# Routing stages: logits by expert in four column tiles, five place products a group, attention rows added one group further ahead

## What is computed

```python
xr = layernorm(x).reshape(-1, 256)
gate = softmax(xr @ Wg, axis=-1)                     # Wg: 256 x 16
idx = argmax(gate, axis=1)
gates_s = take_along_axis(gate, idx[:, None], axis=1)[:, 0]
onehot = one_hot(idx, 16)
loc = sum((cumsum(onehot, axis=0) - 1) * onehot, axis=1)
valid = loc < C                                      # C = 16384 / 16 = 1024
dispatched = zeros((16, C + 1, 256)).at[idx, minimum(loc, C)].set(xr)
```

## Time and profile before

| | us |
|---|---|
| median of 3 runs | 6074.56 |
| lowest and highest run | 6066.26, 6075.16 |
| profiled execution | 6057.65 |
| its span (first to last instruction) | 6056.0 |

### The profile page before, as it was taken

One profiled execution on the slowest core, in us unless ns is written; L12 is line 12 of the kernel. 1 busy time (PEld: TensorE's weight loads), 2 busy tenths in 40 slices (PEclk: granted clock), 3 DMA queues, 4 the chain that ended last, 5 costly groups with the idle time before them and its releaser, 6 DMA issues. The chain is left out here.

```text
span 6056.0 us, 128330 instructions
## 1 busy us (share of the span) xinstructions
PE 5607.2 (93%) x48544; PEld 3845.4 (63%) x48544; DVE 4586.8 (76%) x7474; ACT 3562.4 (59%) x5349; POOL 1574.0 (26%) x2093
## 2 busy tenths in 40 slices
PE   7888867999998979999999999999999997899998
PEld 5666656999987834444444444444444446799998
DVE  6888877556556768888888888888888884755554
ACT  5666533333324547777777777777777775333332
POOL 4666634333330000111111111111111114533333
PEclk9999967999999979999999999999999997799999
DMA  1111184222218921111111111111111113222221
GB/s 49 43 48 48 39 240 125 93 84 85 84 64 284 334 102 45 56 56 55 56 56 57 57 55 56 56 55 55 57 57 56 56 45 95 68 87 83 86 89 56
DMA packets 315523, 495.82 MB, mean 82 GB/s; under 512 B 36314, under 2 KB 221028, under 8 KB 311024
## 3 DMA queue, kind: packets, MB, share of 16 engines
q1 hardware_dynamic: 290544, 425.73, 22.0%
q0 software_dynamic: 24576, 64.56, 3.3%
HBM read 321.82 MB, written 168.82 MB: 81 GB/s over the span
## 5 line engine op out<-in xcount | busy, mean ns | idle before, releaser
L1672 DVE TENSOR_REDUCE at_best<-at_psM 128x2 f32<-128x1024 f32 x2048 | 2409.7, 1220 | 344.7 <-PE at_psM L1716 344.4
L1628 ACT ACTIVATE at_p<-at_psE 128x1024 f32<-128x1024 f32 (+1 forms) x2688 | 2067.7, 819 | 593.0 <-PE at_psE L1732 556.6
L1732 PE MATMUL at_psE<-at_q,at_k 50*128 50x512 f32 x4096 | 1125.8, 428 | 85.0 <-ACT at_p L1628 83.3
L1716 PE MATMUL at_psM<-at_k,at_q 48*128 48x512 f32 x4096 | 1097.5, 455 | 48.0 <-DMA at_v<-scratch_v 26.8
L1742 PE MATMUL at_psO<-at_p,at_v 128*17 128x256 f32 x16384 | 1087.2, 383 | 0.0
L1732 PEld LDWEIGHTS at_psE<-at_q,at_k 50*128 50x128 f32 x4096 | 557.4, 186 | 493.0 <-ACT at_p L1628 245.6
L1053 ACT ACTIVATE e_h_hi<-e_psH 128x512 fp32r<-128x512 f32 x512 | 306.5, 599 | 920.7 <-PE e_psH L90 767.8
L1127 DVE SCALAR_TENSOR_TENSOR e_h_lo<-e_psH,e_h_hi 128x512 fp32r<-128x512 f32 x512 | 353.9, 691 | 602.8 <-ACT e_h_hi L1053 532.4
L1742 PEld LDWEIGHTS at_psO<-at_p,at_v 128*17 128x17 f32 x16384 | 377.8, 97 | 558.8 <-issue 331.5
L1716 PEld LDWEIGHTS at_psM<-at_k,at_q 48*128 48x128 f32 x4096 | 493.5, 187 | 361.6 <-DVE at_best L1672 172.3
L90 PE MATMUL e_psE<-e_w_hi,e_h_hi 128*128 128x256 f32 x2048 | 582.7, 285 | 0.0
(11 more groups left out here) (192 smaller groups left out, 8820.9 us busy)
## 6 DMA issues: line engine op xcount, KB each, us to landing
e_w_raw<-in_w SPq DMA_DIRECT2D x64, 1024.0 KB
scratch_qk<-cp_qkh SPq DMA_DIRECT2D x64, 512.0 KB
scratch_qk<-cp_qkl SPq DMA_DIRECT2D x64, 512.0 KB
at_q<-scratch_qk SPq DMA_DIRECT2D x256, 128.0 KB
at_k<-scratch_qk SPq DMA_DIRECT2D x256, 128.0 KB
scratch_v<-cp_va SPq DMA_DIRECT2D x32, 544.0 KB
at_v<-scratch_v SPq DMA_DIRECT2D x128, 136.0 KB
a_x<-in_x SPq DMA_DIRECT2D x32, 512.0 KB
```

The lines of the kernel that those rows point to most:

```text
L1628: nc.scalar.activation(P[:, u:u + n, :], src, ACT.Exp, scale=HD ** -0.5).then_inc(p_ready, 1)
L1672: nc.vector.reduce_max(best[j % 2][:, h, :, qt], psM[h][:], AX_X).then_inc(m_taken, 1)
L1716: last = nc.tensor.matmul(psM[h][:, a, :], Q[j][r, 128 * qt:128 * qt + 128], K[j][r, 512 * h:512 * h + 512], start=True, stop=True)
L1732: last = nc.tensor.matmul(psE[:, u - u0 if n == 2 else 2, :], K[j][r, 128 * kc:128 * kc + 128], Q[j][r, 512 * half:512 * half + 512], star ...
```

## The change

It touches `routing_stage` only.

- **Logits by expert.** `by_expert` takes the 32 columns of `wg` (16 and 16 zeros) as weights and moves 256 tokens' columns of `r_xT`, for four quarters of the group, each into its own 32 partitions of a new bank `r_psE`: 8 products in place of 16. ScalarE copies `r_psE` to `r_logits_by_expert` (`take_by_expert`), and two transposes bring it back to tokens by experts in `r_psL`, now one buffer in place of two. The tiles of a group then lie as j and half h, and VectorE reads them through a rearranged view. In ScalarE's loop the copy stands first, ahead of `r_expd`; in TensorE's loop the two transposes stand behind the places.
- **Five place products.** VectorE adds tiles in pairs, pairs in fours and fours to the group's count (`r_pairs`, `r_quads`, `r_count`, all in bf16), and the tiles' counts reach later tiles by three products in place of seven.
- **Attention rows.** `add_attention` of group g+5 is done in one piece behind `choose` of g; only the bn_stats of g+4 are left between its steps, one after each.
- The weights `Wg` are loaded last of the first loads, into a tile that GpSimd has cleared.

```diff
@@ buffers
-        wg = sb("wg", [128, 2, E], F32)
+        wg = sb("wg", [128, 2, 32], F32)
+        logits_by_expert = sb("logits_by_expert", [128, G // 4], F32)
...
-        psL = [ps(f"psL{s}", [128, TI, E]) for s in range(2)]
+        psE = ps("psE", [128, G // 4])
+        psL = ps("psL", [128, 2, TI // 2, 32])
@@ SP
-            sp.dma_start(wg[:], Wg.rearrange("(k p) e -> p k e", p=128)).then_inc(wg_loaded, 16)
...
             for q in range(XB):
                 load(q)
+            sp.wait_ge(wg_clear, 1)
+            with nc.allow_non_contiguous_dma(reason="256 rows of 16 weights, once"):
+                sp.dma_start(wg[:, :, 0:E], Wg.rearrange("(k p) e -> p k e", p=128)).then_inc(wg_loaded, 16)
@@ ScalarE
+            def take_by_expert(q):
+                act.wait_ge(by_expert_done, q + 1)
+                after(act, logits_done, q)
+                nc.scalar.activation(logits_by_expert[:], psE[:], ACT.Copy).then_inc(by_expert_taken, 1)
+
             for g in range(-3, NG):
+                if here(g + 1):
+                    take_by_expert(g + 1)
                 if here(g):
@@ VectorE, choose
-                seq.did(nc.vector.tensor_reduce(count[:], onehot[s][:].rearrange("p t e -> p e t"), AX_X, ALU.add))
                 ahead(4)
                 seq.wait(g)
+                two = lambda v: v.rearrange("p (m c) e -> p m c e", c=2)
+                seq.did(nc.vector.tensor_tensor(pairs[:], two(onehot[s][:])[:, :, 0], two(onehot[s][:])[:, :, 1], ALU.add))
+                ahead(5)
+                seq.wait(g)
+                seq.did(nc.vector.tensor_tensor(quads[:], two(pairs[:])[:, :, 0], two(pairs[:])[:, :, 1], ALU.add))
+                ahead(6)
+                seq.wait(g)
+                seq.did(nc.vector.tensor_tensor(count[:], quads[:, 0], quads[:, 1], ALU.add))
+                ahead(7)
+                seq.wait(g)
                 nc.vector.tensor_tensor(counted[1 - s][:], counted[s][:], count[:], ALU.add).then_inc(onehot_ready, 1)
-                ahead(5, 6, 7)
@@ VectorE, loop
-            for g in range(-4, NG):
+            for g in range(-4 if att is None else -5, NG):
...
+                if att is not None and here(g + 5):
+                    add_attention(g + 5)
@@ TensorE
+            def by_expert(q):
+                pe.wait_ge(xT_ready, q + 1)
+                after(pe, by_expert_taken, q)
+                for k in range(2):
+                    for j in range(4):
+                        last = nc.tensor.matmul(psE[32 * j:32 * j + 32, :], wg[:, k, :], xT[q % 2][:, k, G // 4 * j:G // 4 * j + G // 4],
+                                                start=k == 0, stop=k == 1)
+                last.then_inc(by_expert_done, 1)
...
             def logits(q):
-                pe.wait_ge(xT_ready, q + 1)
-                after(pe, below_ready, q - 1)
...
+                pe.wait_ge(by_expert_taken, q + 1)
+                after(pe, below_ready, q)
+                for h in range(2):
+                    last = nc.tensor.transpose(psL[:, h], logits_by_expert[:, 128 * h:128 * h + 128], T.ident[:])
```

More of the change, by code:

```diff
@@ L576, in routing_stage @@
     CE = C // 128
+    assert TI == 8 and E == 16
     assert C % 128 == 0 and N % G == 0 and CH <= 256
@@ L784, in choose @@
                 dve.wait_ge(logits_done, g + 1)
[L785 to L786 removed]
+                by_tile = psL[:].rearrange("p h j e -> p j h e")[:, :, :, 0:E]
+                halves = lambda v: v[:].rearrange("p (j h) -> p j h", h=2)
+                seq.did(nc.vector.reduce_max(halves(mx), by_tile, AX_X))
+                ahead(0)
                 seq.wait(g)
                 after(dve, exp_ready, g)
[L789 to L790 removed]
+                nc.vector.tensor_tensor(below[:].rearrange("p (j h) e -> p j h e", h=2), by_tile,
+                                        halves(mx).unsqueeze(3).broadcast_to([128, TI // 2, 2, E]), ALU.subtract).then_inc(below_ready, 1)
+                ahead(1)
                 dve.wait_ge(below_ready, g + 1)
@@ L794, in choose @@
                                                        op0=ALU.is_equal, op1=ALU.mult))
-                ahead(1)
+                ahead(2)
                 seq.wait(g)
                 seq.did(nc.vector.reduce_max(best[:], marks[:], AX_X))
-                ahead(2)
+                ahead(3)
                 seq.wait(g)
@@ L836, in encode @@
                                         place_row[:].unsqueeze(2).broadcast_to([128, TI, 128]), ALU.is_equal).then_inc(in_row_ready, 1)
-            for g in range(-4, NG):
+            for g in range(-4 if att is None else -5, NG):
                 def ahead(*ts):
                     for t in ts:
-                        if here(g + 4) and t < TI:
+                        if here(g + 4):
                             measure(g + 4, t)
@@ L847, in _ @@
                 else:
-                    ahead(*range(-1, TI))
+                    ahead(*range(TI))
+                if att is not None and here(g + 5):
+                    add_attention(g + 5)
                 if here(g + 4):
@@ L883, in places @@
                 after(pe, codes_ready, g)
-                nc.tensor.matmul(psC[:], earlier[:], onehot[g % 2][:], start=True, stop=False, skip_group_check=True)
-                for t in range(TI - 1):
-                    nc.tensor.matmul(psC[:, t + 1:, :], ones[:], onehot[g % 2][:, t:t + 1, :].broadcast_to([128, TI - 1 - t, E]),
-                                     start=False, stop=False, skip_group_check=True)
+                part = dict(stop=False, skip_group_check=True)
+                hot = onehot[g % 2]
+                nc.tensor.matmul(psC[:], earlier[:], hot[:], start=True, **part)
+                nc.tensor.matmul(psC[:, 4:8], ones[:], quads[:, 0:1].broadcast_to([128, 4, E]), start=False, **part)
+                nc.tensor.matmul(psC[:].rearrange("p (a b c) e -> p a b c e", a=2, b=2)[:, :, 1], ones[:],
+                                 pairs[:].rearrange("p (a b) e -> p a b e", a=2)[:, :, 0].unsqueeze(2).broadcast_to([128, 2, 2, E]), start=False, **part)
+                nc.tensor.matmul(psC[:].rearrange("p (m c) e -> p m c e", c=2)[:, :, 1], ones[:],
+                                 hot[:].rearrange("p (m c) e -> p m c e", c=2)[:, :, 0], start=False, **part)
                 nc.tensor.matmul(psC[:], ones[:], counted[g % 2][:].unsqueeze(1).broadcast_to([128, TI, E]),
@@ L901, in _ @@
                 if here(g + 1):
-                    logits(g + 1)
+                    by_expert(g + 1)
                 if here(g):
                     places(g)
+                if here(g + 1):
+                    logits(g + 1)
                 if here(g + 2):
```

49 lines of the change are left out of this document (19 added, 30 removed).

## The result

| | before | changed |
|---|---|---|
| median, us | 6065.69 (6 runs, 6060.29 to 6075.16) | 6006.71 (6 runs, 6000.92 to 6018.13) |
| profiled execution, its span | 6057.65, 6056.0 | 6003.23, 6001.4 |
| mean granted clock | 0.961 | 0.967 |

The ratio is 0.9902 with a 95% interval of 0.9888 to 0.9916: 59 us faster, where 42 were forecast. 6006.7 lies 9 us under the lower end of the range, so the forecast was right in direction and too small.

What follows compares the result with a forecast made beforehand. VectorE was taken to bound r1 and TensorE r2. Savings of 14.8 us in r1 and 27.5 in r2, together 42.4, came off the median of 6074.56: 6032 us, range 6016 to 6056.

Steps and rivals of the forecast that it cites:

- The burst by expert: TensorE, both routing stages: eight products in four overlapping column tiles take 1.0 us a group in place of 3.64.
- the end of r_picked's wait: VectorE in r2: r_picked no longer waits for the places, taking 1.52 us out of the group's period.
- r_marks and r_onehot: VectorE, both stages: these two-input reads now wait for GpSimd's r_entry products, at 1.2 us each.
- the sixth load: Start of r1: group 1 now stands behind the adds of a sixth load, which lands at 830.8.
- TensorE's need in r2: Per group: table 4.1, burst 1.0, places 0.5, transposes back 0.4, other transposes 3.3, together 9.3 us.
- r2's start: Filling of r2: the first three groups no longer wait for slow logits, so group 2's maxima come 9.6 us earlier.
- both drains: Last three groups of each stage: 9.0, 9.0 and 8.3 us, gaining 5.0 us in r1 and 6.6 in r2.
- r2's tail: Stretch behind r2's last group: 0.15 us longer than before.
- The two periods, 12.5 and 9.95: VectorE's time per group in r1 and r2: 1.3 and 1.15 us less than before.
- r1's fill: Start of r1: the maxima of group 1 come 6.9 us later, at 837.4 in place of 830.56.
- mishaps (tiles, DMA, held reads): Rivals: column tiles don't overlap, 6052 us, chance 0.10; r1 stays at 13.8 through late rows or held reads, 6045, 0.08.
- The rival with the low clock: More idle time keeps TensorE at 1.2 GHz, needing 13.4 us a group; about 35 us slower, 6108 us, chance 0.04.

Runs made afterwards that it cites:

- no_rows_ahead: Changed kernel with the attention additions put back where the kernel before has them; 6021.8 us, ratio 0.9930.
- one_statistic_earlier: On no_rows_ahead, each of the eight bn_stats one place earlier in VectorE's row; 6025.1 us (1 run).
- statistics_early: Changed kernel with a group's eight row statistics issued earlier in VectorE's row, same work; 6001.1 us, run again 5991.6 us.
- narrow_burst: Changed kernel with the old 16 products of 16 columns added behind the logits by expert, result unread; 6100.8 us, ratio 1.0060.
- by_expert_alone: Kernel before with only the logits by expert in four column tiles, ScalarE's copy and two transposes back; 6026.3 us, ratio 0.9939.
- five_places_alone: Kernel before with only the sums of pairs and fours and five place products in place of nine; 6063.8 us, ratio 0.9996.
- rows_ahead_alone: Kernel before with only the eight attention additions together behind the choice, one group further ahead; 6049.6 us, ratio 0.9971.
- filled_chain: On statistics_early, the eight aggregations stand two by two between the four short additions, same work; 6001.9 us, ratio 0.9900.

## Why the prediction was too small

**What held.** Both mechanisms did: the earlier trace rows named the right engine in each stage. The burst by expert (1.0 forecast, 1.07), the two transposes (0.4, 0.39), the copy by ScalarE (0.4, 0.39), the end of r_picked's wait, r_marks and r_onehot (1.2, 1.12 and 1.15), adds that no longer wait, and the sixth load (830.8 forecast, its adds start at 829.22) were right. The rule read from the earlier trace rows, that an instruction of VectorE with two SBUF inputs waits for the end of GpSimd's product, was confirmed three times by moving work around it (no_rows_ahead, one_statistic_earlier, statistics_early). The Trainium skill ("SBUF — State Buffer", SBUF: two separate sides) calls it an exclusive lock. The rows agree: in the earlier trace rows the two products end at 917.43 and what stands behind the held add starts at 917.64, and in the changed kernel (897.06 and 3.85 long, so 900.91) the bn_stats behind r_onehot starts at 900.98.

**What failed, by terms.** The step that failed is the cost of TensorE's other work in r2, which I took at the clock of the kernel before; the second is a pair of periods that were each 0.4 us too long. The saving was 16.6 us short (59.0 against 42.4). The median of before, off which I took it, was 8.9 lower in six runs than in the three that I had, which is the draw of the runs and no step of the argument; taken off the later median, the range would have begun at 6007. Together that makes some 25 us. By the traces the terms were 17.6 short:

- *TensorE's need in r2, "4.1 + 1.0 + 0.5 + 0.4 + 3.3 = 9.3".* It took the table and the transposes at the clock that the earlier trace rows show (0.80 in the group), which the removed burst had held down, as narrow_burst shows by putting it back. Measured 6.80: the burst 1.07, places and the two transposes back 0.4 from start to start where I had 0.5 and 0.4, the transposes 1.91 for 3.3, the table 3.62 for 4.1. The middle of r2 gained nothing by that, since VectorE bounded it anyway; the places where TensorE is waited for did: r2's start (12.3 for 9.6), both drains (rounds of 8.4, 8.1 and 8.1 us for 9.0, 9.0 and 8.3: 6.7 for 5.0, 8.2 for 6.6), r2's tail (1.5 for -0.15, with a last table of 3.69 in place of 5.38). Together some 7.6 us. by_expert_alone has the same start, drain and tail of r2 (45.4, 24.3 and 15.7), so they come with that part. At r2's start the clock is not yet high (0.62 from 5047 to 5076), but the three bursts there took 1.93, 1.07 and 1.36 us where I had twice 1.06 for each. How much of the start's 2.7 us that makes isn't shown. In the drains VectorE hardly waits any more, and 8.1 is what its own work takes; in the kernel before it waited 3.14 us for r_psC in the last group of r2. r1's tail gained 1.4 too, but five_places_alone and rows_ahead_alone, which keep the burst, have the same 15.7, so there it was the clock in that one execution of before.
- *The two periods, 12.5 and 9.95.* Measured 12.13 and 9.51. What is held by the second r_entry product is over 0.19 earlier than I took from r1 of before (the two last 3.85 us together where they lasted 3.98), the three additions take 0.24 of place and not 0.36, and the rest is small gaps of 0.1 to 0.2. Four tenths times some twenty groups are 7.3 us: as much as the first point, from errors of hundredths and tenths that all had one sign. (The prediction's own terms for r2, 4.64 and 5.35, add up to 9.99 and not to 9.95.)
- *r1's fill*, 5.7 for 6.9. The five kernels without the third part have their second maxima 62 to 67 us behind the stage's start, those with it and no added work on TensorE 67 to 70, so 4 to 5 would be the better figure. Each set is spread over some 4 us, so this 1.2 can't be told from chance.

The range was drawn for mishaps (tiles, DMA, held reads) that all lay above the forecast, and for unknown prices of at most 6 us either way. It had no case for "the clock rises when the burst is gone", though the earlier trace rows had a burst that ran 3.64 us at one time and 7.01 at another. The rival with the low clock did note that an always busy TensorE in r2 was granted only 0.80, so that idling could not be the only cause, but it priced idle time alone and didn't look for the other cause; the changed kernel's idle time grew, and the clock rose. (Its 35 us added to 6074.6 give 6110, not 6108.)

One reading was looser than it said: the products on either side of at_psO in the earlier trace rows have 50 rows of weights, not the whole 128x128 array, so that row doesn't hold the switch from whole-array products. The burst's 1.0 us was right all the same, and narrow_burst has the switches that the earlier trace rows lacked.

What stays open: why two products last 3.85 or 3.98 us; and how much of the 4 to 5 us of r1's fill is the sixth load, as against the chance of DMA at that moment. A narrow burst of other width or length wasn't tried, so only the two bursts above are compared.

## What to carry to other kernels

Where a removed burst of narrow products runs beside other TensorE work, cost that other work at the full clock too (here 1.91 us for 3.4 in the transposes), and look for it at the ends of a stage, where TensorE is waited for. On VectorE, put what reads one SBUF tile, or PSUM, ahead of the first instruction with two SBUF inputs while GpSimd works: the wait ends at the same moment whatever stands in front of it, as long as GpSimd's product starts when it did (filled_chain moved that, and lost). When an order is shifted for one reason, go through the row again for what the shift brings elsewhere: here 0.41 us a group in a stage without the moved work.

## What was not expected of the hardware

- With 16 products of 16 columns and 128x128 weights added in each group, the granted clock of a TensorE with hardly any rest fell to 0.50 in most groups (0.81 on average); with 8 products of 128 columns in their place it stayed at 1.00.
- The 16 transposes take 3.62 us at the lower level (903.54, r1 of the changed kernel) and 1.91 at the upper; the table's 8 products take 3.62 at the upper, and 6.16 where all but the end was at the lower (5200.81, r2 of the changed kernel).
- A VectorE instruction with two SBUF inputs that arrives between two GpSimd products slips through in 0.27 us (r_marks at 5114.95, statistics_early); when the second product is under way it waits 1.86 (r_marks at 5085.90, filled_chain).
- Short dependent additions on VectorE cost 0.20 to 0.23 us each back to back and 0.07 to 0.09 with an independent instruction between them.
